# An attention stage where the load of the context for the distance products moves to the front of an iteration's loads

## Chip, cores and metric

The kernel runs on one core of one Trainium2 chip. The metric is device time in microseconds (us), the median of several runs.

## What is computed

The reference is a two-layer gated cross-attention block on 32 batch entries of 256 tokens by 256 features. What matters here, cut short:

```python
x = x + tanh(g_xattn[0]) * L0_xattn(layernorm(x), ctx, ctx)   # 16 heads of 16
x = x + tanh(g_ffn[0]) * L0_ffn(layernorm(x))                 # ternary weights, relu squared
x = x + tanh(g_xattn[1]) * align(ctx, layernorm(x))           # D -> cost table -> path -> add
x = x + tanh(g_ffn[1]) * L1_ffn(layernorm(x))                 # int8-like bitlinear, gelu
```

In `align`, `D` holds the Euclidean distances between the 256 context rows and the 256 rows of the normalised x: `sqrt(aa + bb - 2 * ctx @ x.T)`. The product `ctx @ x.T` is what the text calls the distance product.

## The kernel before, in words

The program has three phases, one after another: an attention phase (the first layer and the distances of the second), an alignment phase (the cost table and the path), and a last phase (the rest of the second layer). The change is in the attention phase.

The attention phase is a software pipeline over 32 batch entries. Each engine has its own hand-written `iteration(i)`, which is called for i from -4 to 33, and the engines meet through semaphores alone. In one iteration the parts belong to different entries: `x` is i+4, `ct` is i+3, `a` is i+2 (projections of queries and keys), `s` is i+1 (first pass of the scores, for the row maxima), `i` itself (second pass of the scores, exponentials, values), `z` is i-1 (output projection, first half of the feed-forward) and `y` is i-2 (second half of the feed-forward, normalisation, distance product).

SyncE (SP) issues every transfer of the phase, in program order on one queue. An iteration's order before the change is: twelve pieces of keys and queries for the second eight heads of `s` (`stack_in`, line 280); the input x of entry `x` (`load_x`, tile `xin`, line 250); x once more for the residual (`load_res`, `xres`, line 254) and the context by tokens (`load_ctx`, `cin`, line 258) of entry `i`; the turned context for the distance products of entry `z` (`load_ctx_products`, `cD_raw`, line 266); the store of the key parts (`parts_out`, line 272), the store of x2 (line 295), the turned context for keys and values (`load_ctx_turned`, `cT_raw`, line 262), the store of the query parts, twelve more pieces for the first eight heads of `a`, the store of the distances (line 300) and the two rows of maxima (`max_rows`, line 290). Each helper waits for its buffer to be free before it issues. For `load_ctx_products` this is

```python
w("d_low", b.n)
sp.dma_start(cD_raw[:], ct_d[b.n].rearrange(feat, p=P)).then_inc(e["cD_in"], 16)
```

`d_low` is counted up by GpSimd (POOL), when `products_low` (line 1137) has read `cD_raw` for the entry before.

ScalarE (ACT) works in order. The part of its iteration around the load is: `ctx_squares` (line 782, reads `cin`); four exponentials of the second score pass (`exps(i, 0, 4)`, line 737, tile `pts`); `products_high` (line 702), which waits for the transfer and copies `cD_raw` into the rounded high part `cDh`; `qh_copy` (line 714); one copy of the value accumulator (line 742); exponentials 4 and 5; `values_copy` (line 729); exponentials 6 and 7; and `yT_copy` (line 746), the high part of the turned y.

VectorE (DVE) then makes the low part of y from that copy (`y_low`, line 959, tile `yTl`). TensorE (PE) runs `scores2` (line 482), among them the pair that needs exponentials 4 and 5 done, the transposes of y and x (line 357), `values(i, 1)` (line 496), which needs exponentials up to 7, and `turn_half` (line 526), which waits for `y_low`. After `turn_half` come the distance product and the whole feed-forward part. The high and low parts made from this load in iteration i are multiplied in iteration i+1: `cD` has two buffers, `cD_raw` has one.

`xin` is read by the statistics of the next iteration (line 928), `cin` by `ctx_squares` and `xres` by `residual1` (line 987) of the next iteration.

Of the kernel before, what the change touches and what calls it, by code (L numbers as in the profile page):

```python
# [103 lines left out]
def attention_phase(nc, io, scr):  # L104
# [3 lines left out]
    with ExitStack() as ctx:  # L108
# [125 lines left out]
        def there(b):  # L234
            return not isinstance(b.n, int) or 0 <= b.n < NB
# [8 lines left out]
        def _(sp):  # L244
            def w(s, count, most=NB):
                done(sp, e[s] if isinstance(s, str) else s, count, most)

            def load_x(b):
                w("ln1", b.n - 1)
                sp.dma_start(xin[b.p][:], x_d[b.n].rearrange(tok, p=P)).then_inc(x_in[b.p], 16)  # L250

            def load_res(b):
                w("x1_res", b.n - 1)
                sp.dma_start(xres[b.p][:], x_d[b.n].rearrange(tok, p=P)).then_inc(xr_in[b.p], 16)

            def load_ctx(b):
                w("aa_sum", T * (b.n - 1), T * NB)
                sp.dma_start(cin[b.p][:], c_d[b.n].rearrange(tok, p=P)).then_inc(c_in[b.p], 16)

            def load_ctx_turned(b):  # L260
                w("c_low", b.n)
                sp.dma_start(cT_raw[:], ct_d[b.n].rearrange(feat, p=P)).then_inc(e["cT_in"], 16)

            def load_ctx_products(b):
                w("d_low", b.n)
                sp.dma_start(cD_raw[:], ct_d[b.n].rearrange(feat, p=P)).then_inc(e["cD_in"], 16)

            def parts_out(b, parts, made, out, dram):
                w(made, b.n + 1)
                for half in range(2):  # L270
                    w(kq_in[1 - b.p][half], 16 * NQ * (b.off(-1).half + 1), 16 * NQ * NB)
                sp.dma_start(dram.rearrange("a (m p) t -> p (a m) t", p=P),
                             parts[:].rearrange("p a m t -> p (a m) t")).then_inc(e[out], 16)

            def stack_in(b, half, out, dram, st, order):
                w("s2_mm", NH * (b.n - 2) + NH // 2 * (half + 1), NH * NB)
                w(out, 16 * (b.n + 1), 16 * NB)
                heads = slice(NH // 2 * half, NH // 2 * (half + 1))
                for blk, part in enumerate(order):
                    sp.dma_start(st[b.p][DH * blk:DH * blk + DH, heads, :],  # L280
                                 dram[part].rearrange("(h r) t -> r h t", r=DH)[:, heads, :])\
                        .then_inc(kq_in[b.p][half], 16)

            def max_rows(b):
                w("max_split", b.n + 1)
                w("s2_mm", NH * (b.n - 1), NH * NB)
                if b.n < 2:
                    sp.wait_ge(e["pool_set"], PADS_SET + b.n)
                for part in range(2):
                    sp.dma_start(qst[b.p][MAXROW + part:MAXROW + part + 1, :, :].rearrange("o h (a t) -> o (h a) t", t=P),  # L290
                                 nsp[:, part:part + 1, :].rearrange("m o t -> m o t")).then_inc(e["max_in"], 16)

            def store_x2(b):
                w("x2_res", b.n + 1)
                sp.dma_start(scr["x2"][b.n].rearrange(tok, p=P), x2[:]).then_inc(e["x2_out"], 16)

            def store_d(b):
                w("dist", b.n + 1)
                for t in range(T):
                    sp.dma_start(scr["d"].rearrange("k b (t p) c -> p t b k c", p=P)[:, t, b.n, :, :],  # L300
                                 dd[:, t, :].rearrange("p (k c) -> p k c", c=BW)).then_inc(e["d_out"], 16)
# [16 lines left out]
            def iteration(i):  # L318
                s, a, ct, x, z, y = i.off(1), i.off(2), i.off(3), i.off(4), i.off(-1), i.off(-2)
                if there(s):  # L320
                    stack_in(s, 1, "k_out", scr["k"], kst, K_PARTS)
                    stack_in(s, 1, "q_out", scr["q"], qst, Q_PARTS)
                if there(x):
                    load_x(x)
                if there(i):
                    load_res(i)
                    load_ctx(i)
                if there(z):
                    load_ctx_products(z)
                if there(a):  # L330
                    parts_out(a, kp, "k_parts", "k_out", scr["k"])
                if there(y):
                    store_x2(y)
                if there(ct):
                    load_ctx_turned(ct)
                if there(a):
                    parts_out(a, qp, "q_parts", "q_out", scr["q"])
                    stack_in(a, 0, "k_out", scr["k"], kst, K_PARTS)
                if there(y):
                    store_d(y)  # L340
                if there(a):
                    stack_in(a, 0, "q_out", scr["q"], qst, Q_PARTS)
                if there(s):
                    max_rows(s)
            unrolled(iteration, {-4: weights_straight, -3: weights_ffn})
            sp.wait_ge(e["x2_out"], 16 * NB)
            sp.wait_ge(e["d_out"], 16 * T * NB)
# [1625 lines left out]
```

## Time and profile before

| | |
|---|---|
| median of 3 runs | 1813.73 us (1809.11 to 1814.77) |
| profiled execution, span from the first to the last instruction | 1810.7 us |
| busy share of the span | PE 76%, DVE 82%, ACT 63%, POOL 36% |
| granted TensorE clock, attention phase, 100 to 1000 us | 1.00 |
| transfers in the span | 179.56 MB, mean 99 GB/s |

The page gives the profiled execution by its span and lists no other time of its own. The attention phase takes the first 1120 us or so, the alignment phase is the stretch where PE's share falls, and the last phase the final third. A busy share over the whole span mixes these. Rows of the timeline read: start in us, duration in us, engine, line, operation, tile written <- tiles read, shape, count, and in brackets the idle time of the engine just before and what ended it. Adjacent instructions of one line are merged into one row with a count. "SPq" rows are the issue of a transfer, not the transfer.

### The profile page before, as it was taken

The page shows a single profiled execution, that of the slowest core. Times are in us where ns is not written, and L with a number is a line of the kernel's source. Part 1 is how long each engine was busy: PE and PEld are TensorE (multiplying, and loading weights), DVE is VectorE, ACT ScalarE, POOL GpSimd, SP SyncE. Part 2 cuts the span into 40 slices and gives each one's busy share as a digit, 9 for nine tenths or more (in the row PEclk, how much of TensorE's full clock was granted, in tenths as well). Part 3 has the DMA queues.
Part 4 walks back from the last instruction along what each step waited for, and adds up shares of the span by engine and source line. Part 5 has one row for each costly group of instructions (what it writes and reads, how often), then busy time and mean ns, then how long its engine had stood idle before and what let it go on. Part 6 is the DMA issues. An engine that isn't in the chain of part 4 may idle for free. (4 is left out here: it accounts for less than half of the span.)

```text
span 1810.7 us, 37501 instructions
## 1 busy us (share of the span) xinstructions
PE 1379.4 (76%) x11461; PEld 1067.0 (59%) x11461; DVE 1489.1 (82%) x4194; ACT 1135.9 (63%) x2463; POOL 644.9 (36%) x1094
## 2 busy tenths in 40 slices
PE   4899999999999999999999984233332004899996
PEld 4577878888888888888888764000001003666664
DVE  7777877878878787788877753999998998999995
ACT  4567677776777767777677662243334002999997
POOL 3333343433434334343343322200000003787785
PEclk7999999999999999999999996555555556999999
DMA  6444544445444454444544311322220002223321
GB/s 173 137 128 115 149 123 118 137 122 154 123 117 139 120 154 123 118 141 122 152 125 120 99 36 28 96 60 61 60 42 8 0 0 84 74 89 98 96 77 48
DMA packets 322942, 179.56 MB, mean 99 GB/s; under 512 B 93793, under 2 KB 318193, under 8 KB 322802
## 3 DMA queue, kind: packets, MB, share of 16 engines
q1 hardware_dynamic: 322802, 178.07, 35.2%
q8 instruction: 42, 0.69, 0.2%
q14 instruction: 98, 0.80, 0.1%
HBM read 122.91 MB, written 50.33 MB: 96 GB/s over the span
## 5 line engine op out<-in xcount | busy, mean ns | idle before, releaser
L1031 DVE TENSOR_REDUCE nmax<-s 128x2 f32<-128x512 f32 x512 | 327.5, 681 | 7.6 <-PE s L465 6.6
L737 ACT ACTIVATE pts<-s 128x512 f32<-128x512 f32 x512 | 282.3, 617 | 75.0 <-PE s L482 74.8
L1143 POOL TENSOR_TENSOR r<-rl 128x512 f32<-128x512 f32 x128 | 133.4, 1042 | 260.8 <-ACT rl L767 217.9
L465 PE MATMUL s<-kst,qst 96*128 96x256 bf16 x1024 | 158.7, 276 | 10.9 <-DVE nmax L1031 6.9
L482 PE MATMUL s<-qst,kst 128*128 128x256 bf16 x1024 | 160.3, 276 | 8.7 <-ACT pts L737 7.2
L1421 PE MATMUL gate<-diag,one 128*128 128x512 f16 x35 | 21.2, 607 | 171.9 <-DVE left L1512 171.9
L767 ACT ACTIVATE rl<-wb,fscl 128x256 f32<-128x256 f32 x256 | 108.0, 477 | 64.8 <-PE wb L568 64.8
L564 PE MATMUL wb<-x2l,wfcT 128*128 128x256 f32 x512 | 143.3, 302 | 0.7 <-ACT dd L789 0.7
L1000 DVE TENSOR_TENSOR r2l<-r,r2h 128x512 fp32r<-128x512 f32 x128 | 88.6, 692 | 66.0 <-POOL r L1143 40.3
L496 PE MATMUL oacc<-pts,vw 128*32 128x256 f32 x2048 | 137.9, 387 | 5.3 <-ACT pts L737 5.2
L431 PE MATMUL wb<-wprT,r2l 128*128 128x256 f32 x512 | 130.5, 293 | 6.9 <-DVE r2l L1000 6.9
L565 PE MATMUL wb<-x2h,wfcT 128*128 128x256 f32 x512 | 132.6, 281 | 0.0
L1537 DVE SCALAR_TENSOR_TENSOR hop<-iota,path,steps 32x256 f32<-32x256 f32 x255 | 120.7, 473 | 12.4 <-DMA steps<-step 3.4
L432 PE MATMUL wb<-wprT,r2h 128*128 128x256 f32 x512 | 124.5, 282 | 0.0
L482 PEld LDWEIGHTS s<-qst,kst 128*128 128x128 bf16 x1024 | 82.3, 98 | 58.7 <-ACT pts L737 29.3
L1421 PEld LDWEIGHTS gate<-diag,one 128*128 128x128 f16 x35 | 3.6, 104 | 189.3 <-DVE left L1512 175.6
L465 PEld LDWEIGHTS s<-kst,qst 96*128 96x128 bf16 x1024 | 91.3, 98 | 30.1 <-DVE nmax L1031 12.3
L1713 ACT ACTIVATE apart<-iota,mid 128x256 f32<-128x256 f32 x64 | 28.7, 509 | 124.3 <-DVEq L1919 118.9
L431 PEld LDWEIGHTS wb<-wprT,r2l 128*128 128x128 f32 x512 | 97.7, 191 | 13.9 <-DVE r2l L1000 7.9
L1154 POOL TENSOR_TENSOR ln_y<-ln_v,ln_pow 128x4 f32<-128x4 f32 (+1 forms) x37 | 34.5, 932 | 196.5 <-DVE ln_v L1067 196.2
L1499 DVE TENSOR_TENSOR_SCAN rows_r<-best,rows_r,rows_d 128x64 f32<-128x64 f32 x280 | 100.3, 358 | 0.7 <-ACT rows_r L1357 0.3
L1357 ACT ACTIVATE rows_r<-rows_r 32x8 f32<-32x8 f32 x102 | 21.9, 215 | 123.3 <-DVE rows_r L1499 122.5
(304 smaller groups left out, 4630.9 us busy)
## 6 DMA issues: line engine op xcount, KB each, us to landing
kst<-k_parts_dram SPq DMA_DIRECT2D x384, 64.0 KB, 2.6
qst<-q_parts_dram SPq DMA_DIRECT2D x384, 64.0 KB, 2.4
k_parts_dram<-kp SPq DMA_DIRECT2D x32, 384.0 KB, 5.4
q_parts_dram<-qp SPq DMA_DIRECT2D x32, 384.0 KB, 3.1
xin<-in_x_dram SPq DMA_DIRECT2D x32, 256.0 KB, 2.8
cT_raw<-in_ctx_T_dram SPq DMA_DIRECT2D x32, 256.0 KB, 5.4
xres<-in_x_dram SPq DMA_DIRECT2D x32, 256.0 KB, 3.1
cin<-in_ctx_dram SPq DMA_DIRECT2D x32, 256.0 KB, 4.7
```

Of the source, the lines that this page charges most:

```text
L431: pe.matmul(B_PROJ[:, t, :], r2l[:, f, t * P:t * P + P], wprT[:, f, :], start=(f == 0), stop=False)
L432: last = pe.matmul(B_PROJ[:, t, :], r2h[:, f, t * P:t * P + P], wprT[:, f, :], start=False, stop=(f == FT - 1))
L465: last = pe.matmul(s1[h % 2][:, t, :], qst[b.p][0:MAXROW, h, t * P:t * P + P], kst[b.p][0:MAXROW, h, :], start=True, stop=True)
L482: last = pe.matmul(s2[h % 2][:, t, :], kst[b.p][:, h, t * P:t * P + P], qst[b.p][:, h, :], start=True, stop=True)
L496: last = pe.matmul(oacc[HW * j:HW * j + HW, g % 2, :], vw[b.p][:, t, HPG * g + j, :], pt[(HPG * g + j) % (2 * HPG)][:, t, :], start=(t == ...
L564: pe.matmul(B_FC[k][:, j, :], wfcT[:, c, f * P:f * P + P], x2l[:, c, :], start=(c == 0), stop=False)
L565: pe.matmul(B_FC[k][:, j, :], wfcT[:, c, f * P:f * P + P], x2h[:, c, :], start=False, stop=False)
L737: act.activation(pt[h % (2 * HPG)], s2[h % 2][:], ACT.Exp).then_inc(e["expd"], 1)
L767: last = act.activation(rl[:, k % 2, j, :], B_FC[k][:, j, :], ACT.Relu, scale=fscl[:, 2 * k + j:2 * k + j + 1])
L1031: v.tensor_reduce(nmax[:, T * h:T * h + T], s1[h % 2][:], AX.X, ALU.max, negate=True)\
L1143: pool.tensor_tensor(r2[:], rl[:, k % 2], rl[:, k % 2], ALU.mult)\
L1537: ch.link(v.scalar_tensor_tensor(hop[:], iota[:], path[:, i + 1:i + 2], steps[:, i, :], ALU.is_le, ALU.mult, accum_out=path[:, i:i + 1]))
```

## The change

The call of `load_ctx_products` moves up by three issues, from behind `load_ctx` to a place before `load_x`. Nothing else changes: the same transfers are issued, with the same waits of their own.

```diff
                 if there(s):
                     stack_in(s, 1, "k_out", scr["k"], kst, K_PARTS)
                     stack_in(s, 1, "q_out", scr["q"], qst, Q_PARTS)
+                if there(z):
+                    load_ctx_products(z)
                 if there(x):
                     load_x(x)
                 if there(i):
                     load_res(i)
                     load_ctx(i)
-                if there(z):
-                    load_ctx_products(z)
                 if there(a):
                     parts_out(a, kp, "k_parts", "k_out", scr["k"])
```

## Rows read from the trace of the kernel before

**Rows 1.** Windows: stretch, length, busy per engine, clock, DMA share, GB/s

```profile
500.00:600.00 100.00, 98.56 (x911) 82.59 (x911) 79.94 (x176) 72.22 (x165) 38.06 (x52) 1.00 0.44 127
```

**Rows 2.** Waits from 100 to 1040 us: total us, times, longest

```profile
ACT cDh L702 <- DMA cD_raw<-in_ctx_T_dram: 86.8, 29, 4.7
```

**Rows 3.** Timeline, one iteration with a usual wait: ACT, DVE, PE

```profile
548.08 0.63 ACT L702 ACTIVATE cDh<-cD_raw 128x512 fp32r<-128x512 f32 x1 [3.22 <-DMA cD_raw<-in_ctx_T_dram]
...
551.79 0.67 ACT L746 ACTIVATE yTh<-wb 128x512 fp32r<-128x512 f32 x1
...
552.49 0.69 DVE L959 TENSOR_TENSOR yTl<-wb,yTh 128x512 fp32r<-128x512 f32 x1 [0.70 <-ACT yTh L746]
...
553.44 0.30 PE L526 MATMUL wb<-ident,hpart 128*128 128x128 f32 x1 [0.27 <-DVE yTl L959]
...
576.23 1.09 ACT L737 ACTIVATE pts<-s 128x512 f32<-128x512 f32 x2 [1.68 <-PE s L482]
```

**Rows 4.** Timeline, an iteration without the x load, with a short wait

```profile
960.29 0.43 SPq L254 DMA_DIRECT2D xres<-in_x_dram  x1
...
962.00 0.47 SPq L266 DMA_DIRECT2D cD_raw<-in_ctx_T_dram  x1
...
965.63 0.63 ACT L702 ACTIVATE cDh<-cD_raw 128x512 fp32r<-128x512 f32 x1 [1.72 <-DMA cD_raw<-in_ctx_T_dram]
...
970.47 0.60 ACT L746 ACTIVATE yTh<-wb 128x512 fp32r<-128x512 f32 x1
971.10 0.69 DVE L959 TENSOR_TENSOR yTl<-wb,yTh 128x512 fp32r<-128x512 f32 x1 [0.27 <-ACT yTh L746]
...
972.05 0.30 PE L526 MATMUL wb<-ident,hpart 128*128 128x128 f32 x1 [0.15 <-issue]
...
994.85 1.09 ACT L737 ACTIVATE pts<-s 128x512 f32<-128x512 f32 x2 [1.69 <-PE s L482]
```

**Rows 5.** SP's queue in the iteration of rows 3: four loads as issued

```profile
541.30 0.43 SPq L250 DMA_DIRECT2D xin<-in_x_dram  x1
541.77 0.47 SPq L254 DMA_DIRECT2D xres<-in_x_dram  x1
542.28 0.47 SPq L258 DMA_DIRECT2D cin<-in_ctx_dram  x1
543.09 0.37 SPq L266 DMA_DIRECT2D cD_raw<-in_ctx_T_dram  x1
```

**Rows 6.** DMA issues, whole span: KB each, median us from issue to landing

```profile
xin<-in_x_dram SPq DMA_DIRECT2D x32, 256.0 KB, 2.8
...
cD_raw<-in_ctx_T_dram SPq DMA_DIRECT2D x32, 256.0 KB, 4.8
```

**Rows 7.** Line 526 from 128 to 1010 us: group, first and last

```profile
L526 PE MATMUL wb<-ident,hpart x28: 299/300/331, 129.9 to 1004.1; 128*128 128x128 f32 x28
...
129.87 0.30 PE L526 MATMUL wb<-ident,hpart 128*128 128x128 f32 x1 [0.35 <-DVE yTl L959]
...
1004.08 0.30 PE L526 MATMUL wb<-ident,hpart 128*128 128x128 f32 x1 [0.28 <-DVE yTl L959]
```

**Rows 8.** Timeline, the first iteration that has the load

```profile
86.24 0.43 SPq L250 DMA_DIRECT2D xin<-in_x_dram  x1
...
92.61 0.63 ACT L702 ACTIVATE cDh<-cD_raw 128x512 fp32r<-128x512 f32 x1 [5.81 <-DMA cD_raw<-in_ctx_T_dram]
...
94.55 0.88 PE L482 MATMUL s<-qst,kst 128*128 128x256 bf16 x4 [2.37 <-ACT pts L737]
```

**Rows 9.** Windows: the stretch just behind that iteration's stall

```profile
96.00:100.00 4.00, 3.44 (x24) 1.99 (x25) 1.88 (x3) 2.73 (x7) 2.41 (x3) 0.57 0.08 22
```

**Rows 10.** Timeline, the last iteration in which ACT waits for the load

```profile
1030.86 0.63 ACT L702 ACTIVATE cDh<-cD_raw 128x512 fp32r<-128x512 f32 x1 [3.55 <-DMA cD_raw<-in_ctx_T_dram]
```

**Rows 11.** Timeline, behind rows 3: reader of `cD_raw`, next reader of `cin`

```profile
554.66 1.30 POOL L1137 TENSOR_TENSOR cDl<-cD_raw,cDh 128x512 fp32r<-128x512 f32 x1
...
571.77 0.40 ACT L782 ACTIVATE junk<-cin 128x256 f32<-128x256 f32 x1
```

## The prediction

> **What bounds the kernel now.** I first read the windows view, to separate the stages. In the attention phase TensorE is busy 98.56 of 100 us by its modelled ends, at the full granted clock of 1.00, while VectorE has 79.94 and ScalarE 72.22 [rows 1]. The phase therefore looks bound by TensorE, and only what holds TensorE up can be won. The wait view then names the change's own subject: ScalarE waits for the context of the distance products 29 times between 100 and 1040 us, 86.8 us in all, 3.0 us each, at most 4.7 [rows 2]. ScalarE is not the bound, so these 86.8 us are a ceiling and not a forecast. What counts is how much of each wait reaches TensorE.
>
> For that I followed one iteration through the timeline [rows 3]. ScalarE has finished its exponentials and arrives at line 702 at 548.08 - 3.22 = 544.86; the data land and it goes on at 548.08. What was queued behind then runs in one piece until the copy of y at 551.79; VectorE, which waited 0.70 for that copy, makes its low part at 552.49, and TensorE's line 526 can start at 553.44. That is 5.36 us from the end of the wait to line 526, and 8.58 from ScalarE's arrival.
>
> Now the same steps where no x load was issued ahead, so that the transfer stood one place further forward [rows 4]. The wait is 1.72 instead of 3.22. ScalarE arrived at 965.63 - 1.72 = 963.91, and line 526 started at 972.05, 8.14 after the arrival. A wait shorter by 1.50 made line 526 earlier by only 0.44: other work sets a **floor of 8.14 us**. A wait is free up to 8.14 - 5.36 = 2.78 us, and only what exceeds 2.78 delays TensorE.
>
> Does the delay stay? From line 526 to ScalarE's next arrival, the end of the pair of exponentials, it is 576.23 + 1.09 - 553.44 = 23.88 us behind the long wait and 994.85 + 1.09 - 972.05 = 23.89 behind the short one [rows 3, 4]. The rest of an iteration follows line 526 rigidly and catches nothing up, so each saved microsecond should reach the end.
>
> **The change, part by part.** One transfer of 256 KB moves past three issues on SP's queue; nothing is added or removed. SP's issues stand about 0.5 us apart, and the place of the x load is at 541.30, that of the moved one at 543.09: 1.79 us earlier [rows 5]. On the DMA side, the transfer at the head of the four lands a median 2.8 us after its issue, the one at the end 4.8 us, both of 256 KB [rows 6]. I take the head's 2.8 for the moved transfer, since it takes exactly that place behind the same twelve pieces; the bounds are 2.8 and 4.8. It should then land at 541.30 + 2.8 = 544.1, 0.8 us before ScalarE arrives, against 3.2 us after it. Even 4.8 gives 546.1, a wait of 1.2, still below the free 2.78.
>
> *Steady state.* With all waits below the floor an iteration takes the time between two lines 526 behind short waits, 1004.08 - 972.05 = 32.03 us [rows 4, 7]. The 28 starts of line 526 from 129.87 to 1004.08 hold 27 iterations, 874.21 us, 32.38 each [rows 7]. The saving is 874.21 - 27 x 32.03 = **9.4 us**. The floor's rows differ by hundredths (8.14 + 23.89 = 32.03), so I bound this term by 8.4 and 10.
>
> *Start.* In the first iteration with this load ScalarE waits 5.81 us and TensorE 2.37 us for it [rows 8]. At the head, the load would be issued at 86.24 and land at 89.0, so ScalarE would go on 3.5 us sooner. TensorE gains between its own 2.37 and those 3.5, plus what the slow clock costs: behind the stall, between 96 and 100 us, the mean granted clock is 0.57, nearly all at the 1.2 GHz level, after a stretch in which TensorE stood still [rows 9]; four microseconds at 0.57 lose up to 1.7. The bounds are 2.4 and 5.2; I take **3.5**, as in the rows both the idle time and part of the slow clock should go. The Trainium skill, "TensorE: Matmul & The Clock Gate", Part 1, says that the throttled clock is the resting state and that activity releases it; by that rule the whole 1.7 would come back with a shorter stall, and the start would be worth 5.2, within the bounds.
>
> *End.* The last iteration with a wait has 3.55, of which 3.55 - 2.78 = **0.8** exceeds the floor [rows 10]; bounds 0 and 1.4. Later loads are not waited for.
>
> *What the move is past.* Three loads are issued one place later. The last of them lands, at worst in the old last place, at 543.09 + 4.8 = 547.9; the context by tokens is next read at 571.77 [rows 5, 6, 11], 23.9 us later, and the two x loads are also read an iteration later. Cost: nothing; if that cover were gone, each would cost its lateness once an iteration. The transfer's own wait, for POOL's reading of the buffer, now stands before the three loads, the store of the key parts and all that follows on SP. POOL ends that reading at 554.66 + 1.30 = 555.96 [rows 11], while SP reaches the new place 32.03 us after 541.30, at 573.3: 17.4 us of slack, cost nothing. ScalarE's copy moves into a stretch where it stood idle; what is late next is the copy of y, which then hangs on TensorE's score pair and two exponentials, as behind the short wait.
>
> The sum is 9.4 + 3.5 + 0.8 = **13.7 us**. The profiled execution's span of 1810.7 would become 1797.0. The median of the runs shown stands 3.0 above that span, at 1813.73, so 1813.73 - 13.7 = **1800.0 us**, 0.76% less.
>
> **Rivals.**
>
> *The floor gives way too (8%).* Behind the short wait VectorE still stood idle 0.27 us for the copy of y [rows 4]. If an earlier transfer also brought that copy forward, 28 x 0.27 = 7.6 us more would go: 1792.4. Against it: ScalarE was already back in step there, and its copy followed TensorE's scores, not the load.
>
> *The head is no early place (5%).* The twelve pieces in front may hold it as the four loads did. By the 4.8 us of the last place the steady 9.4 stays, since 1.2 is below 2.78, but the start lands at 91.0, only 1.6 us sooner: 9.4 + 1.6 + 0.4 = 11.4, with half of the end's term, and 1802.3. Against it: the x load stands behind the same pieces and lands in 2.8. The Trainium skill, "DMA: Bandwidth & Descriptors", section "Queues, rings and completion order", speaks for this rival: a completion increment lands only after every earlier write of that DMA engine, so the pieces ahead would still count. The 2.8 of the x load contains whatever that costs.
>
> *Absorbed (8%).* Another wait takes the freed time in the steady state, and only start and end remain: 4.3 us, 1809.4. For it: TensorE's busy share leaves but 1.44 us in 100 [rows 1], 13 us over 900. Against it: 23.88 and 23.89 after line 526, and line 526 itself waits in both.
>
> *Slower (2%).* The wait for POOL now heads SP's loads. If POOL read the buffer over 17.4 us later than now, SP would stand there and hold everything behind. It decides for slower from the point where the load lands later than today, 3.2 us after ScalarE's arrival: 544.86 + 3.22 - 2.8 = 545.3 for the issue, so another 4.0 us behind the new place, 21.4 in all. Each further 0.2 an iteration is 5.6 us over 28: 1819. That the change does nothing (the wait keeps the load where it was) falls between these two and is counted under absorbed. No row shows SP waiting there.
>
> **How the numbers follow.** The forecast has 77%, the rivals 8, 5, 8 and 2. Its own bounds are 8.4 + 2.4 + 0 = 10.8 and 10 + 5.2 + 1.4 = 16.6 us, so 1802.9 to 1797.1. The runs shown reach 4.6 below their median and 1.0 above; with that the range is 1793 to 1805, a little over at the upper end for the second rival. It leaves out the first, third and fourth rival, 18%. About 0.3%, 5.4 us, is what a measurement of this kernel can tell from no change. Forecast and the first two rivals are all faster by more, 90%; I give 0.87 for scatter, 0.10 for no difference and 0.03 for slower.
>
> **What would show it.** In the changed kernel's profile the wait of line 702 should nearly vanish from the wait view; the load should be issued first of the four and land in about 2.8 us, the context by tokens in about 4.8; line 526 should start 8.1 us after ScalarE's arrival in all iterations, with 32.0 between them; the first iteration's TensorE stall should be below 1 us. If line 526 stays at 8.5, another wait took over and I am wrong; if it falls below 8.0, the floor was not one.

## The result, and the profile after

The changed kernel takes 1802.18 us in the median of 5 runs (1798.45 to 1804.86), the kernel before 1813.73 us in the median of 5 runs beside it (1809.11 to 1818.67). The ratio is 0.9935, with a 95% interval of 0.9916 to 0.9953: faster by 0.65%, or 11.6 us, where 13.7 us and 1800.0 us were forecast. The profiled execution took 1802.82 us in all; its span is 1801.0 us, against 1810.7 before.

The timeline of the changed kernel, in the same iteration as [rows 3, 5], all engines mixed (columns as in the rows before):

```profile
532.52 0.43 SPq L266 DMA_DIRECT2D cD_raw<-in_ctx_T_dram  x1
532.99 0.47 SPq L250 DMA_DIRECT2D xin<-in_x_dram  x1
533.51 0.47 SPq L254 DMA_DIRECT2D xres<-in_x_dram  x1
534.31 0.37 SPq L258 DMA_DIRECT2D cin<-in_ctx_dram  x1
535.00 1.09 ACT L737 ACTIVATE pts<-s 128x512 f32<-128x512 f32 x2 [1.68 <-PE s L482]
535.97 0.63 ACT L702 ACTIVATE cDh<-cD_raw 128x512 fp32r<-128x512 f32 x1
...
538.07 0.60 ACT L714 ACTIVATE qp<-wb 128x512 bf16<-128x512 f32 x1 [1.47 <-PE wb L363]
...
542.65 0.61 ACT L746 ACTIVATE yTh<-wb 128x512 fp32r<-128x512 f32 x1
543.29 0.69 DVE L959 TENSOR_TENSOR yTl<-wb,yTh 128x512 fp32r<-128x512 f32 x1 [0.27 <-ACT yTh L746]
...
544.24 0.30 PE L526 MATMUL wb<-ident,hpart 128*128 128x128 f32 x1 [0.15 <-issue]
```

Line 702 has no bracket any more: it runs straight behind the exponentials, which end at 535.00 + 1.09 = 536.09. The 3.22 us in which ScalarE stood there [rows 3] became 1.47 us in front of line 714, which waits for TensorE and costs nothing. From 536.09 to line 526 it is 8.15 us, against 8.58 before and 8.14 behind the short wait [rows 3, 4]. VectorE's 0.27 in front of line 959 is also that of [rows 4]: this is the floor, now in an ordinary iteration.

The wait view from 100 to 1040 us: the load, 86.8 us in 29 waits before [rows 2], is nearly gone, and ScalarE's wait for the query product takes its place, off the path.

```profile
ACT qp L714 <- PE wb L363: 40.2, 28, 1.5
...
ACT cDh L702 <- DMA cD_raw<-in_ctx_T_dram: 1.2, 2, 1.0
```

The transfers of the phase, KB each and median us from issue to landing [rows 6]:

```profile
xin<-in_x_dram SPq DMA_DIRECT2D x32, 256.0 KB, 3.1
...
xres<-in_x_dram SPq DMA_DIRECT2D x32, 256.0 KB, 4.5
cin<-in_ctx_dram SPq DMA_DIRECT2D x32, 256.0 KB, 4.8
cD_raw<-in_ctx_T_dram SPq DMA_DIRECT2D x32, 256.0 KB, 2.8
```

The landing goes with the place, not with the tensor: the moved load has the x load's 2.8, the context by tokens the 4.8 of the last place. And line 526 from the 1st to the 28th start [rows 7]:

```profile
L526 PE MATMUL wb<-ident,hpart x28: 298/300/329, 127.5 to 992.5; 128*128 128x128 f32 x28
...
127.51 0.30 PE L526 MATMUL wb<-ident,hpart 128*128 128x128 f32 x1
...
992.53 0.30 PE L526 MATMUL wb<-ident,hpart 128*128 128x128 f32 x1 [0.28 <-DVE yTl L959]
```

These are 865.02 us for 27 iterations, 32.04 each, where it was 874.21 and 32.38.

### The profile page after: what moved, and what is told of

Same layout as the page of the kernel before. It is cut to its first block and busy times, and to the rows that moved or that the text cites. A ratio compares the mean times of both kernels' runs of the same rounds, so it can differ in the third digit from the quotient of the medians.

```text
span 1801.0 us, 37501 instructions
## 1 busy us (share of the span) xinstructions
PE 1376.1 (76%) x11461; PEld 1069.3 (59%) x11461; DVE 1489.2 (83%) x4194; ACT 1144.5 (64%) x2463; POOL 644.3 (36%) x1094
## 5 line engine op out<-in xcount | busy, mean ns | idle before, releaser
L1143 POOL TENSOR_TENSOR r<-rl 128x512 f32<-128x512 f32 x128 | 133.2, 1040 | 258.5 <-ACT rl L767 215.6
L465 PE MATMUL s<-kst,qst 96*128 96x256 bf16 x1024 | 158.5, 276 | 10.3 <-DVE nmax L1031 6.7
L1537 DVE SCALAR_TENSOR_TENSOR hop<-iota,path,steps 32x256 f32<-32x256 f32 x255 | 120.7, 473 | 12.4 <-DMA steps<-step 3.4
L432 PEld LDWEIGHTS wb<-wprT,r2h 128*128 128x128 f32 x512 | 99.7, 195 | 0.0
```

The lines of the kernel that those rows point to most:

```text
L432: last = pe.matmul(B_PROJ[:, t, :], r2h[:, f, t * P:t * P + P], wprT[:, f, :], start=False, stop=(f == FT - 1))
L465: last = pe.matmul(s1[h % 2][:, t, :], qst[b.p][0:MAXROW, h, t * P:t * P + P], kst[b.p][0:MAXROW, h, :], start=True, stop=True)
L1143: pool.tensor_tensor(r2[:], rl[:, k % 2], rl[:, k % 2], ALU.mult)\
L1537: ch.link(v.scalar_tensor_tensor(hop[:], iota[:], path[:, i + 1:i + 2], steps[:, i, :], ALU.is_le, ALU.mult, accum_out=path[:, i:i + 1]))
```

## The experiments

The question was whether the prediction's mechanism is the cause: ScalarE stands in order in front of the copy, and only what exceeds 2.78 us of that wait reaches TensorE. The rivals were that any part of the wait costs, that the order of the transfers itself brought the time, and that the floor yields to a still earlier load. "us per iteration" below is always the distance from the 1st to the 28th start of line 526, divided by 27.

**The load one place up.**

```diff
                 if there(i):
                     load_res(i)
+                if there(z):
+                    load_ctx_products(z)
+                if there(i):
                     load_ctx(i)
-                if there(z):
-                    load_ctx_products(z)
```

> The load moves up by one place only: behind the x and residual loads, ahead of the context by tokens. Threshold theory (a wait costs only what exceeds 2.78 us): the load then lands where the context by tokens landed before, about 2.1 us after ScalarE's arrival instead of 3.0, which is below 2.78, so line 526 starts 8.1 to 8.2 us after the arrival in nearly all iterations and nearly the whole steady saving of 9.2 us is there; with about 1 us at the start the median is about 10 us below the kernel before. Rival (the saving goes with the length of the wait): 0.9 of 3.0 us of the wait is gone, so 30% of the steady saving, 3 us, and 1 us at the start: 4 us below before.

Measured: 1806.55 us, ratio 0.996 (0.9947 to 0.9972) against 1814.41 for before. Wait view and line 526 (line numbers here are one higher):

```profile
ACT cDh L703 <- DMA cD_raw<-in_ctx_T_dram: 61.8, 29, 3.6
```

```profile
L527 PE MATMUL wb<-ident,hpart x28: 298/301/329, 131.8 to 997.5; 128*128 128x128 f32 x28
```

The waits are still 2.13 us on average, 71% of the 2.99 before, yet an iteration takes 865.7 / 27 = 32.06 us: 93% of the steady saving is there with 29% of the wait gone. That is the threshold, and it rules out the proportional rival. The median is 7.9 us below that of before, 2.1 short of the 10 expected; in the profile the first line 526 stands at 131.8 instead of 129.9. This run's ScalarE reached the first copy 4.2 us later than in the profile before (90.96 against 86.80), ahead of any moved load, so at least that profile's shortfall lies in the start.

**The load one place down.**

```diff
                     load_ctx(i)
-                if there(z):
-                    load_ctx_products(z)
                 if there(a):
                     parts_out(a, kp, "k_parts", "k_out", scr["k"])
+                if there(z):
+                    load_ctx_products(z)
```

> The load moves down by one place, behind the store of the key parts (384 KB). Threshold theory: the wait grows from 3.0 to about 4.5 us, all of the growth is above the free 2.78, and each iteration takes it whole: line 526 about 10 us after ScalarE's arrival, 28 x 1.4 = 39 us slower than before (25 to 55 with the uncertainty of the wait). Rival (the saving goes with the length of the wait, 9.2 us for 86.8 us of wait): 28 x 1.5 x 0.11 = 5 us slower.

Measured: 1831.52 us, ratio 1.0103 (1.0084 to 1.0122), 17.1 us slower than before.

```profile
ACT cDh L702 <- DMA cD_raw<-in_ctx_T_dram: 103.5, 28, 5.1
```

```profile
L526 PE MATMUL wb<-ident,hpart x28: 298/300/303, 134.1 to 1022.4; 128*128 128x128 f32 x28
```

Neither number (39 us, 25 at the least, and 5 us) came, because the wait grew to 103.5 / 28 = 3.70 us and not to 4.5: the store of the keys held the load up less than assumed. With the wait that there was, the threshold asks for 3.70 - 2.78 = 0.92 us above the floor, 32.04 + 0.92 = 32.96 us per iteration; 888.3 / 27 = 32.90 were measured (the 28 waits include one ahead of the first start, of 5.04). From 2.99 to 3.70 us of wait the iteration grew by 0.52, while from 2.99 down to 2.13 it shrank by 0.32 and from there to nothing by 0.02. Per iteration the excess before was 0.34, more than 2.99 - 2.78, since the waits scatter around the threshold and only the longer ones count. Taken wait by wait from the traces, what exceeds 2.78 us adds up over the 27 iterations to 8.7 us before, 0.7 one place up and 23.4 one place down; the 27 iterations took 9.2, 0.7 and 23.3 us longer than those of the changed kernel. So the threshold gives the size in all three, from one number read before the change.

**The load at the very head**, ahead of the twelve pieces; the edit is against the changed kernel.

```diff
+                if there(z):
+                    load_ctx_products(z)
                 if there(s):
                     stack_in(s, 1, "k_out", scr["k"], kst, K_PARTS)
                     stack_in(s, 1, "q_out", scr["q"], qst, Q_PARTS)
-                if there(z):
-                    load_ctx_products(z)
```

> The load moves further up, ahead of the iteration's twelve pieces of keys and queries. Floor theory: it lands some 9 us ahead of ScalarE's arrival, but 8.14 us and 32.03 us per iteration stay as in the changed kernel; only the first iteration with the load loses its remaining wait of 2.0 us: 0 to 2 us below the changed kernel. Rival (the floor gives way when the load is early enough): 0.2 us an iteration more, 6 us below the changed kernel. A cost would show as waits for the second eight heads' pieces in the first score pass, which now land about 0.5 us later; more than 10 us of cover are there, so none is expected.

Measured: 1801.09 us, ratio 0.9929 (0.9915 to 0.9944).

```profile
L526 PE MATMUL wb<-ident,hpart x28: 299/301/329, 125.7 to 990.7; 128*128 128x128 f32 x28
```

No wait for the load is left at all, and an iteration takes 865.0 / 27 = 32.04 us. The load now lands about 6 us ahead of ScalarE's arrival (9 were expected), and the time of an iteration has not moved by a hundredth. The rival that the floor gives way is out. The ratio's interval covers the 0.9935 of the changed kernel.

**ScalarE's copy later, SP's order as before.** The first attempt put the copy ahead of the fourth relu and POOL's low part behind its squares.

```diff
-                if there(z):
-                    products_high(z)
...
                     copy_group(i, 3)
                 if there(z):
+                    products_high(z)
                     relu(z, 3)
...
-                if there(z):
-                    products_low(z)
                 if there(ct):
                     ctx_low(ct)
                 if there(z):
                     squares(z)
+                    products_low(z)
```

> SP's order stays that of the kernel before, the load at its old last place. Instead ScalarE's copy moves to a stretch late in the iteration where ScalarE stands idle 0.6 us (ahead of the fourth relu), with POOL's low part behind its four squares, so that nobody waits for the load. Theory of the prediction (what cost time was ScalarE standing in front of work in its order): line 526 at 8.1 us after the arrival, 32.03 us per iteration, and a median like that of the changed kernel, 11 to 13 us below before. Rival (the changed order of the transfers brought the time, through the loads that now come later): no saving, within 3 us of before.

Measured: 1838.84 us, ratio 1.0135 (1.0117 to 1.0153), 24 us slower, which neither theory expected. The wait for the load was gone as planned, but an iteration took 33.12 us, 1.08 above the floor. The timeline showed an instruction that had grown by 1.06 (line numbers here are one lower):

```profile
575.72 1.28 POOL L1136 TENSOR_TENSOR cDl<-cD_raw,cDh 128x512 fp32r<-128x512 f32 x1
575.79 1.75 DVE L999 TENSOR_TENSOR r2l<-r,r2h 128x512 fp32r<-128x512 f32 x1 [0.84 <-POOL r L1142]
```

VectorE's subtraction of two SBUF tiles, 0.69 us elsewhere, took 1.75: it started 0.07 behind POOL's operation and ended 0.54 behind it. It is the last of an iteration's four such subtractions. The next iteration's proj (line 431) waits for it and for `xTl`, which VectorE makes right behind it; the wait view has TensorE standing there nearly 1 us an iteration,

```profile
PE wb L431 <- DVE xTl L950: 23.6, 24, 1.0
...
PE wb L431 <- DVE r2l L999: 4.0, 4, 1.0
```

where the changed kernel has 1.3 us in all. Two kernels took this apart.

**Only POOL's part late**, on the changed kernel:

```diff
-                if there(z):
-                    products_low(z)
                 if there(ct):
                     ctx_low(ct)
                 if there(z):
                     squares(z)
+                    products_low(z)
```

> The changed kernel with one difference: POOL's low part of the distance products stands behind its four squares, as in the late copy; ScalarE's copy stays. Theory (POOL's operation and VectorE's line 1000 shut each other out): one of four line 1000 an iteration takes 1.75 us instead of 0.69, an iteration 33.1 us, about 1.06 x 29 = 31 us slower than the changed kernel. Rival (the late copy was slow because of ScalarE's or TensorE's own order): line 1000 at 0.69, no difference from the changed kernel.

Measured: 1836.49 us, ratio 1.0121 (1.0105 to 1.0136), 35.9 us slower than the changed kernel's 1800.60 in the same set of runs, a little more than the 31 expected, at 33.12 us per iteration. The same pair again:

```profile
573.17 1.28 POOL L1137 TENSOR_TENSOR cDl<-cD_raw,cDh 128x512 fp32r<-128x512 f32 x1
573.24 1.75 DVE L1000 TENSOR_TENSOR r2l<-r,r2h 128x512 fp32r<-128x512 f32 x1 [0.84 <-POOL r L1143]
```

Nothing but POOL's place differs from the changed kernel, so the slowdown is due to that place alone.

**The copy later, without that collision**: SP's order as before, the copy ahead of the first relu, POOL's low part, which reads the copy, ahead of its squares.

```diff
                 if there(i):
                     exps(i, 0, 4)
-                if there(z):
-                    products_high(z)
...
                     exps(i, 8, 10)
                 if there(z):
+                    products_high(z)
                     relu(z, 0)
...
-                if there(z):
-                    products_low(z)
                 if there(ct):
                     ctx_low(ct)
                 if there(z):
+                    products_low(z)
                     squares(z)
```

> As the late copy, with SP's order of the kernel before, but at another place: ScalarE's copy stands ahead of the first relu, where ScalarE was idle 1.05 us, and POOL's low part ahead of its squares, where POOL was idle 2.4 us and VectorE reads PSUM. Theory (ScalarE standing in front of its queue was the cost, and the late copy lost its gain only because POOL's low part ran beside VectorE's line 1000 and held it 1.06 us an iteration): 32.03 to 32.1 us between lines 526, line 1000 back at 0.69 us at most, a median 10 to 13 us below before. Rival (the order of the transfers brought the gain): no gain, within 3 us of before.

Measured: 1802.15 us, ratio 0.9922 (0.9908 to 0.9935), 12.8 us below its 1814.96 for before, at 865.5 / 27 = 32.06 us per iteration.

```profile
L526 PE MATMUL wb<-ident,hpart x28: 299/301/328, 124.9 to 990.4; 128*128 128x128 f32 x28
```

```profile
L999 DVE TENSOR_TENSOR r2l<-r,r2h x128: 691/692/694, 100.6 to 1096.7; 128x512 fp32r<-128x512 f32 x128
```

The whole gain, with the transfers issued in the old order. The order on SP was never the cost; ScalarE standing in front of its queue was.

**The gap of the floor filled**, on top of the very head:

```diff
                 if there(i):
                     values(i, 1)
+                    scores2(i, 8, 10)
                 if there(y):
                     turn_half(y)
                     products(y)
                 if there(z):
                     low_rank(z)
-                if there(i):
-                    scores2(i, 8, 10)
```

> The very head for the load, and on TensorE the ninth and tenth second-pass score matmuls ahead of line 526, where TensorE still stands idle 0.2 us for the low part of y. Theory (the floor of 8.14 us is TensorE waiting for the chain scores, exponentials, copy of y, low part of y): TensorE fills the gap, an iteration takes 0.15 to 0.25 us less, 31.8 us, and the median is 4 to 7 us below the very head's. Rival (ScalarE's or VectorE's later work sets the pace as well): 32.03 us stay, the same median.

Measured: 1805.06 us, ratio 0.995 (0.9936 to 0.9963), so behind the very head; 32.21 us per iteration, 0.17 more. The score pair had covered another wait, that of the first feed-forward product for the low-rank part, which now shows in the wait view of this kernel

```profile
PEld wb L568 <- DVE lowt L1010: 15.5, 29, 0.5
...
PE wb L568 <- DVE lowt L1010: 9.6, 29, 0.3
```

and is not in the changed kernel's. A miss: this pair was not spare. Whether other work would fill the gap was not tried.

**The changed kernel again**, with no edit.

> The changed kernel again, for a second profile. Theory (the clock in the run-out of the attention phase and the first iterations' times vary from run to run, the steady state doesn't): 32.04 us an iteration to a hundredth; the run-out from the 28th line 526 to the last, 119.2 us in the first profile against 117.9 before, may come out either way; median within 3 us of 1802. Rival (the move costs the run-out 1.3 us each time): 119.2 again.

Measured: 1800.60 us, ratio 0.9925 (0.9911 to 0.9938), at 32.04 us per iteration.

```profile
L526 PE MATMUL wb<-ident,hpart x28: 298/301/331, 126.7 to 991.9; 128*128 128x128 f32 x28
```

The run-out, from the 28th to the last line 526, took 118.1 us here, 119.2 in the first profile and 117.9 before: it varies, and a cost of 1.3 us each time is out. The stretch from the 28th to the 29th start holds the saving at the end, though; from the 29th to the last it is 87.4 us here, 88.4 in the first profile and 86.2 before, so these three alone do not exclude a smaller cost.

## Why the prediction was right

*Landing.* Right: 2.8 us at the head, 4.8 at the end.

*Floor of 8.14 and threshold of 2.78.* Right, and shown from both sides: one place up, 71% of the wait remains and costs almost nothing; one place down, the iteration grows by what exceeds the threshold; six more us of lead change nothing, and summed wait by wait the threshold gives the size in all three kernels.

*Steady state, 9.4 us.* Measured 874.21 - 865.02 = 9.2. It is not spread evenly: the first three of the 27 iterations had the longest waits,

```profile
158.40 0.63 ACT L702 ACTIVATE cDh<-cD_raw 128x512 fp32r<-128x512 f32 x1 [4.70 <-DMA cD_raw<-in_ctx_T_dram]
...
191.77 0.63 ACT L702 ACTIVATE cDh<-cD_raw 128x512 fp32r<-128x512 f32 x1 [4.13 <-DMA cD_raw<-in_ctx_T_dram]
...
225.18 0.63 ACT L702 ACTIVATE cDh<-cD_raw 128x512 fp32r<-128x512 f32 x1 [4.17 <-DMA cD_raw<-in_ctx_T_dram]
```

and gave 4.5 us together; the other 24 gave about 0.2 each. The sum over the 27 starts was right because it held both kinds.

*Start, 3.5 us between 2.4 and 5.2.* From ScalarE's first arrival at the copy to the first line 526 it took 129.87 - 86.80 = 43.1 us before, 127.51 - 88.01 = 39.5 after, and 126.70 - 88.60 = 38.1 in the second profile of the changed kernel: 3.6 and 5.0. ScalarE's first wait fell from 5.81 us to 1.98 and 2.33,

```profile
89.99 0.64 ACT L702 ACTIVATE cDh<-cD_raw 128x512 fp32r<-128x512 f32 x1 [1.98 <-DMA cD_raw<-in_ctx_T_dram]
```

```profile
90.93 0.63 ACT L702 ACTIVATE cDh<-cD_raw 128x512 fp32r<-128x512 f32 x1 [2.33 <-DMA cD_raw<-in_ctx_T_dram]
```

(the second line is of the second profile), and TensorE's 2.37 us are gone. So is the slow clock behind the stall [rows 9], with 1.00 where it was 0.57:

```profile
96.00:100.00 4.00, 3.56 (x38) 2.79 (x39) 3.10 (x6) 3.40 (x8) 2.79 (x3) 1.00 0.17 48
```

By the rule of the Trainium skill, "TensorE: Matmul & The Clock Gate", Part 1, the whole 1.7 us would come back, 5.2 in all; the second profile comes near that, the first does not. The first has a slow stretch of its own a little earlier, with a granted clock of 0.50 (the 1.2 GHz level) from 87 to 90 us, where the second has 1.00:

```profile
87.00:90.00 3.00, 3.00 (x16) 3.00 (x15) 1.36 (x4) 1.02 (x3) 0.70 (x1) 0.50 0.73 212
```

The 2.0 us of it behind ScalarE's arrival at 88.01 lose 1.0 of the 1.4 us between the two profiles. Both have the same TensorE waits of 1.19, 0.21, 0.42 and 0.20 us shortly ahead of it, so why only one slowed down stays open.

*End, 0.8 us.* From the 28th to the 29th line 526 it is 1023.29 - 992.53 = 30.76 us after, 1035.74 - 1004.08 = 31.66 before: 0.9. A wait of 0.98 us for the load is left there, and it is free.

*The sum, 13.7, against 11.6 of the medians and 9.7 of the profiled spans.* The three terms as measured are 9.2 + 3.6 + 0.9 = 13.7, so the mechanism and its sizes held. What did not hold is an unspoken step, that everything ahead of the first wait and behind the last stays the same. Ahead of it the profiled execution of the changed kernel reached the first copy 88.01 - 86.80 = 1.2 us later. At the last proj of the attention phase it was 1081.26 - 1068.84 = 12.4 us ahead. There its matmuls slowed down to the lower clock, and those of the kernel before did not, although TensorE had waited the same 0.87 us in both (before first):

```profile
1081.26 0.39 PE L431 MATMUL wb<-wprT,r2l 128*128 128x256 f32 x1 [0.87 <-DVE r2l L1000]
```

TensorE's timeline of the changed kernel:

```profile
1068.84 0.38 PE L431 MATMUL wb<-wprT,r2l 128*128 128x256 f32 x1 [0.87 <-DVE r2l L1000]
...
1069.41 0.28 PE L431 MATMUL wb<-wprT,r2l 128*128 128x256 f32 x1
1069.53 0.33 PE L432 MATMUL wb<-wprT,r2h 128*128 128x256 f32 x1
1069.65 0.42 PE L431 MATMUL wb<-wprT,r2l 128*128 128x256 f32 x1
1069.87 0.42 PE L432 MATMUL wb<-wprT,r2h 128*128 128x256 f32 x1
```

Starts 0.12 us apart become 0.22 apart. In views of 10 us the granted clock is 0.83 for this stretch in the changed kernel,

```profile
1066.00:1076.00 10.00, 8.13 (x53) 7.45 (x51) 3.61 (x8) 3.49 (x9) 1.04 (x1) 0.83 0.00 0
```

and 1.00 for the same work before and in the second profile of the changed kernel:

```profile
1077.00:1087.00 10.00, 8.00 (x66) 7.29 (x62) 4.30 (x8) 4.14 (x11) 1.87 (x2) 1.00 0.00 0
```

```profile
1065.00:1075.00 10.00, 8.32 (x74) 7.40 (x66) 3.86 (x7) 4.58 (x12) 2.08 (x2) 1.00 0.00 0
```

(the first of these two of the kernel before, the second of the changed one's second profile). By the last line 526 the lead was 1121.98 - 1111.70 = 10.3 us, and 9.7 at the end of the span. In the second profile the low level came at another place, 1035 to 1045 us, with 0.83 there, where the kernel before has 1.00 for the same work. Whether the move has a part in this is not settled, but the other profiles speak for scatter: from the 29th to the last line 526 they took 86.7 us with the load one place up, 87.8 at the very head, 86.3 there with the gap filled, and 88.2 one place down, where the load comes later than before. So the time does not follow the load's place. ScalarE's first arrival also scatters by some 4 us, 86.80 to 90.96, before a moved load can matter; with these the single spans cannot settle a last microsecond or two, and the second set of runs gives 1814.96 - 1800.60 = 14.4 us for the same pair of kernels. The forecast lies between the 11.6 and the 14.4; which of the two it comes nearer to is chance, as such scatter is not in its sum.

*The rivals.* The floor did not give way, the head was an early place, nothing absorbed the gain, and SP waited at its new place for nothing that the wait view shows.

## What to carry to other kernels

A wait on an engine that is not the bound has a free part: compare iterations of one trace in which the same wait is long and short, take the time from the engine's arrival to the bound's next instruction in both, and price only what exceeds the floor. Price it wait by wait and not by the mean: here three waits of 27 held half of the gain. ScalarE worked through its instructions in order, so the wait could be removed by an earlier transfer or by a later reader, and both gave the same (32.04 and 32.06 us per iteration); but a moved instruction brings its own collisions, and idle time is not all equally free.

## What was not expected of the hardware

POOL's subtraction of two SBUF tiles and VectorE's subtraction of two SBUF tiles do not run side by side: started 0.07 us behind POOL's 1.28 us, VectorE's 0.69 became 1.75 us, in each of the 27 iterations between 100 and 1000 us of both kernels that let them meet, and cost 1.08 us per iteration (33.12 against 32.04), 35.9 us in all where nothing else differed. A smaller VectorE subtraction, `lowt<-wb,lowt`, takes one of its two inputs from PSUM (`wb`). In the changed kernel the first of a pair of these runs inside a POOL subtraction of the same kind and keeps its 0.42 us; the pair takes 0.86:

```profile
546.70 1.27 POOL L1132 TENSOR_TENSOR cTl<-cT_raw,cTh 128x512 fp32r<-128x512 f32 x1
...
547.53 0.86 DVE L1011 TENSOR_TENSOR lowt<-wb,lowt 32x256 fp32r<-32x256 f32 x2 [1.76 <-ACT lowt L754]
```

The Trainium skill, "SBUF — State Buffer", section "Who interferes with whom", says that a VectorE instruction with two SBUF inputs contends with a GpSimd instruction that reads SBUF, and that the shared port pair is an exclusive lock for which the order of issue decides who blocks. The traces agree: POOL, issued first, kept its 1.28 us, and VectorE ended 0.54 us behind it.
